# Self-attention in two row halves, the residual added by TensorE, and idle products on TensorE, in a three-stage transformer kernel

## The reference

```
x = x + cross_attention(context, layernorm(x))       # 16 heads of 16, masked by lengths
h = layernorm(x)
x = x + LN( h + softmax(causal(q k^T / 16) + bias) v @ proj + proj_b ) * ln_g + ln_b
g = layernorm(x)
x = x + down( qdq( qdq(g_gate * sigmoid(g_gate)) * g_up ) )  # weights in 4 bits by blocks of 32,
                                                             # activations in 16 bits by one scale
```

## Time and profile before

| | us |
|---|---|
| median of 3 runs (lowest, highest) | 1663.82 (1662.29, 1664.6) |
| the profiled execution | 1663.34 |
| its span in the trace | 1661.2 |
| TensorE busy, products | 1419.8 (85%) |
| VectorE busy | 1079.0 (65%) |
| ScalarE busy | 890.3 (54%) |
| GpSimd busy | 839.5 (51%) |

### The profile page before, as it was taken

How to read it: one execution, slowest core, us unless ns; L and a number is a source line. 1 busy time by engine, 2 the same in 40 slices (tenths; PEclk the granted TensorE clock), 3 DMA queues, 4 the chain that set the end, 5 groups by cost and what they waited for, 6 DMA issues and landing times. The chain is left out here.

```text
span 1661.2 us, 54781 instructions
## 1 busy us (share of the span) xinstructions
PE 1419.8 (85%) x24061; PEld 990.7 (60%) x24061; DVE 1079.0 (65%) x1743; ACT 890.3 (54%) x1170; POOL 839.5 (51%) x557
## 2 busy tenths in 40 slices
PE   4789999999999999999999999999975477448508
PEld 2357777776777777667777766777753255323207
DVE  7756666666666666666666666666633468885984
ACT  1446666565566655556665555666555244234752
POOL 5567666555666655556665556666302477211000
PEclk9899999999999999999999999999997678678859
DMA  5553354444344444433444443345303520010001
GB/s 169 128 143 102 102 122 124 110 129 124 102 102 121 122 116 115 135 102 103 117 123 116 115 139 102 102 117 126 73 14 110 138 54 9 1 38 1 0 0 52
DMA packets 91916, 158.55 MB, mean 95 GB/s; under 512 B 17488, under 2 KB 56280, under 8 KB 91680
## 3 DMA queue, kind: packets, MB, share of 16 engines
q1 hardware_dynamic: 90320, 154.07, 35.6%
q10 hardware_dynamic: 1360, 0.98, 0.2%
HBM read 60.95 MB, written 2.20 MB: 38 GB/s over the span
## 5 line engine op out<-in xcount | busy, mean ns | idle before, releaser
L638 DVE TENSOR_REDUCE MXP<-W_PS 128x1 f32<-128x512 f32 x768 | 499.1, 687 | 284.6 <-PE W_PS L450 284.6
L534 ACT ACTIVATE PR<-S_PS 128x1024 f32<-128x1024 f32 (+1 forms) x416 | 424.9, 1023 | 259.9 <-PE S_PS L398 252.0
L344 POOL TENSOR_TENSOR K_HI<-K,MCOL 128x512 f16<-128x512 f32 (+1 forms) x224 | 219.5, 980 | 426.7 <-ACT K L542 425.4
L346 POOL TENSOR_TENSOR K_LO<-K,K_HI 128x512 f16<-128x512 f32 (+1 forms) x224 | 291.9, 1303 | 17.6
L450 PE MATMUL W_PS<-STK,QS 105*128 105x512 f16 (+1 forms) x1024 | 269.8, 335 | 9.0 <-POOL STK L371 4.8
L398 PE MATMUL S_PS<-QS,STK 105*128 105x128 f16 (+1 forms) x3328 | 256.1, 220 | 1.0 <-DVE QS L652 1.0
L413 PE MATMUL O_PS<-PR,V 128*17 128x64 f32 x13312 | 231.3, 220 | 8.4 <-ACT PR L534 7.5
L413 PEld LDWEIGHTS O_PS<-PR,V 128*17 128x17 f32 x13312 | 190.8, 97 | 79.4 <-issue 59.3
L433 PE MATMUL W_PS<-WV_HI,CTX_HI 128*128 128x256 f16 (+1 forms) x832 | 228.3, 274 | 1.6 <-DVE WV_LO L611 1.4
L398 PEld LDWEIGHTS S_PS<-QS,STK 105*128 105x128 f16 (+1 forms) x3328 | 201.3, 99 | 45.3 <-issue 1.3
L433 PE MATMUL W_PS<-WV_HI,CTX_LO 128*128 128x256 f16 (+1 forms) x832 | 227.8, 274 | 0.0
(11 more groups left out here) (239 smaller groups left out, 1600.0 us busy)
## 6 DMA issues: line engine op xcount, KB each, us to landing
CTX<-in_ctx_t SPq DMA_DIRECT2D x64, 800.5 KB, 5.9
STK<-K_HI SPq DMA_DIRECT2D x256, 128.0 KB, 2.5
STK<-K_HI SPq DMA_DIRECT2D x256, 72.1 KB, 2.1
STK<-K_LO SPq DMA_DIRECT2D x128, 128.0 KB, 2.6
STK<-K_LO SPq DMA_DIRECT2D x128, 72.1 KB, 2.1
QSTK<-STK SPq DMA_DIRECT2D x12, 192.0 KB
V<-T SPq DMA_DIRECT2D x2, 1024.0 KB, 10.0
SQS<-QK_HI SPq DMA_DIRECT2D x32, 64.0 KB, 2.1
```

The lines of the kernel that those rows point to most:

```text
L344: pool.tensor_tensor(K_HI[:, m, lo:hi], k32, zero, ALU.add).then_inc(k_hi, 1)
L346: pool.tensor_tensor(K_LO[:, m, lo:hi], k32, K_HI[:, m, lo:hi], ALU.subtract).then_inc(k_lo, 1)
L534: nc.scalar.activation(PR[0:m, par, :], S_PS[par][0:m, :], ACT.Exp).then_inc(p_sb, 1)
L638: dve.tensor_reduce(MXP[:, j, at:at + 1], bank[:, :], AX.X, ALU.max).then_inc(mx_done, 1)
```

## The change

**Heads.** SQS and SKS have 128 rows. Transfers write every fourth row: rows q, q+4, ... hold part q of a head pair, so the even head lies in rows 0 to 63 and the odd one in rows 64 to 127; every fourth row from 3 on is zero. A block's scores are 32 products of 64 rows and 64 columns in place of 16 of 96 rows and 128 columns, and S_PS holds the even heads first. A round has 24 transfers. For round 0 ScalarE issues the eight with the keys' high part.

**Zeros.** Two transfers zero the rows of SQS and SKS; VectorE clears V by memsets; `zero_keys` goes.

**Values.** ScalarE copies V (`values`). VV of round 1 moves from SETUP to steps 1 and 2, QK, TN and WT units are spread anew.

**Residual.** TensorE adds it and the bias row: a product of the identity with XN, one of a row of ones with BP, then the projection. ScalarE copies the sum to XN behind the exponential of the step. GpSimd's four bias sums go.

**ScalarE's order.** Units come behind the exponential.

**Gate weight.** It has memory of its own (WN) and is loaded and prepared ahead of step 0.

**Norms.** Groups are 0 to 7, 8 to 12, 13 to 15. For blocks 0 to 7 ScalarE centres and scales (`centred`, steps 12 and 13), GpSimd multiplies by the weight (steps 13, 14) and VectorE adds four blocks at once (`add_weighted`).

**Idle products.** 12 ahead of SETUP, 8 ahead of the gate units and 8 ahead of the down projection, 400 columns each, results unused.

```diff
 SETUP = [
     ("TN", 0, 0), ("TN", 0, 1), ("QK", 0, 0), ("QK", 0, 1), ("QK", 0, 2), ("QK", 0, 3), ("TN", 1, 0), ("TN", 1, 1),
-    ("VV", 0, 0), ("VV", 0, 1), ("QK", 1, 0), ("QK", 1, 1), ("QK", 1, 2), ("QK", 1, 3), ("VV", 1, 0), ("VV", 1, 1),
+    ("VV", 0, 0), ("VV", 0, 1), ("QK", 1, 0), ("QK", 1, 1), ("QK", 1, 2), ("QK", 1, 3),
 ]
 BESIDE = {
-    0: [("TN", 2, 0), ("TN", 2, 1)], 1: [("QK", 2, 0), ("QK", 2, 1)], 2: [("QK", 2, 2), ("QK", 2, 3)],
-    3: [("TN", 3, 0), ("TN", 3, 1)], 4: [("QK", 3, 0), ("QK", 3, 1)], 5: [("QK", 3, 2), ("QK", 3, 3)],
-    6: [("VV", 2, 0)], 7: [("VV", 2, 1)], 8: [("WT", 0, 0), ("WT", 0, 1)], 9: [("WT", 0, 2), ("WT", 0, 3)],
-    10: [("VV", 3, 0)], 11: [("VV", 3, 1)],
-    16: [("XT", 0, 0), ("XT", 0, 1)], 17: [("XT", 1, 0), ("XT", 1, 1), ("XT", 2, 0)],
+    0: [("TN", 2, 0), ("TN", 2, 1)], 1: [("QK", 2, 0), ("VV", 1, 0)], 2: [("QK", 2, 1), ("VV", 1, 1)], 3: [("QK", 2, 2)],
+    4: [("QK", 2, 3), ("TN", 3, 0), ("TN", 3, 1)], 5: [("QK", 3, 0)], 6: [("QK", 3, 1), ("VV", 2, 0)], 7: [("QK", 3, 2), ("VV", 2, 1)],
+    8: [("QK", 3, 3)], 9: [("WT", 0, 0), ("WT", 0, 1)], 10: [("VV", 3, 0), ("WT", 0, 2)], 11: [("VV", 3, 1), ("WT", 0, 3)],
+    16: [("XT", 0, 0), ("XT", 0, 1)], 17: [("XT", 1, 0), ("XT", 1, 1)],
 }
-ENDING = [("XT", 2, 1), ("XT", 3, 0), ("XT", 3, 1)]
+ENDING = [("XT", 2, 0), ("XT", 2, 1), ("XT", 3, 0), ("XT", 3, 1)]
 STEPS = TILES + 3
 WIDE = 4
 NARROW = 2
-RESIDUAL = {0: 0, 1: 1, 4: 2, 7: 3}
-NORMS = [(0, 10), (10, 14), (14, 16)]
-ADDED = {13: (0, 1, 2), 14: (3, 4, 5), 15: (6, 7, 8), 16: (9,)}
+WARM = 12
+NORMS = [(0, 8), (8, 13), (13, 16)]
 CHAIN = 12
-AGGREGATED = [10, 20, 24, 28, 30, 32]
+AGGREGATED = [8, 16, 21, 26, 29, 32]
 ROOT_GUESS = 1597463007.0
-MAXIMA = [(0, 4), (4, 8), (8, 10), (10, 14), (14, 16)]
+MAXIMA = [(0, 4), (4, 8), (8, 13), (13, 16)]
...
-    SQS = alloc("SQS", [96, 2, PAIRS, CH], F16)
-    KZ = alloc("KZ", [96, 2, PAIRS, 2, CH], F16)
+    SQS = alloc("SQS", [P, 2, PAIRS, CH], F16)
+    SKS = alloc("SKS", [P, 2, PAIRS, CH], F16)
     T = alloc("T", [P, 3, PAIRS, 2, SQ], F32)
     MX = alloc("MX2", [P, 2, PAIRS, 2], F32)
     SM = alloc("SM2", [P, 2, PAIRS, 2], F32)
     PT = alloc("PT2", [P, 2, PAIRS, P], F32)
     OT = alloc("OT2", [P, 2, KT, P], F32)
+    WN = alloc("WN2", [P, WCOLS], F32)[:, :]
+    ONE = alloc("ONE", [1, P], F32)
...
+    zeroed = sem(nc, ctx, "zeroed")
+    PARTS = 24
...
+    def stack(eng, r, dst, q, part, m):
+
+        for c in range(4):
+            eng.dma_start(dst[q:P:4, r % 2, c::4, :], part[32 * c:32 * c + 32, r % 2, m:m + 2, :]).then_inc(stacked[r], 16)
...
+        sp.dma_start(WN.rearrange("p (f d) -> p f d", f=FT), dram["w_gate"].rearrange("(f p) d -> p f d", p=P)).then_inc(sm["in_wg"], 16)
         sp.wait_ge(sm["zero"], 1)
...
+        for home in (SQS, SKS):
+            sp.dma_start(home[3:P:4].rearrange("p u j c -> p (u j c)").bitcast(F32).rearrange("p (n z) -> p n z", n=4),
+                         ZERO[0:32].unsqueeze(1).broadcast_to([32, 4, PAIRS * 2 * SQ])).then_inc(zeroed, 16)
...
             sp.wait_ge(sm["qk_hi"], 4 * r + 2)
             if r >= 2:
                 sp.wait_ge(sm["s_ps"], 4 * (r - 1))
-            queries(0, QK_HI)
-            queries(1, QK_HI)
-            sp.wait_ge(sm["qk_hi"], 4 * r + 4)
-            if r == 0:
-                sp.wait_ge(sm["zero"], 5)
-            elif r == 1:
-                sp.wait_ge(zeroed[1], 32)
-            keys(0, QK_HI)
-            keys(2, QK_HI)
+            stack(sp, r, SQS, 0, QK_HI, 0)
+            stack(sp, r, SQS, 1, QK_HI, 0)
+            if r:
+                sp.wait_ge(sm["qk_hi"], 4 * r + 4)
+                stack(sp, r, SKS, 0, QK_HI, 2)
+                stack(sp, r, SKS, 2, QK_HI, 2)
+            sp.wait_ge(sm["qk_lo"], 4 * r + 2)
+            stack(sp, r, SQS, 2, QK_LO, 0)
             sp.wait_ge(sm["qk_lo"], 4 * r + 4)
-            queries(2, QK_LO)
-            keys(1, QK_LO)
-            if r == 1:
-                sp.wait_ge(sm["w_hi"], 1)
-                sp.wait_ge(sm["w_lo"], 1)
-                sp.dma_start(WN.rearrange("p (f d) -> p f d", f=FT), dram["w_gate"].rearrange("(f p) d -> p f d", p=P))\
-                    .then_inc(sm["in_wg"], 16)
+            stack(sp, r, SKS, 1, QK_LO, 2)
...
@@ -1031,27 +1008,30 @@
         def scores(t):
 
             r, lo = t // 4, t % 4 * P
+            if t == 0:
+                pe.wait_ge(zeroed, 32)
...
             for j in range(PAIRS):
                 for w in range(2):
                     cols = slice(lo + w * SQ, lo + (w + 1) * SQ)
-                    last = pe.matmul(S_PS[SQ * w:SQ * (w + 1), j * P:(j + 1) * P], SQS[0:96, r % 2, j, cols],
-                                     KZ[0:96, r % 2, j, :, cols], start=True, stop=True, skip_group_check=True)
+                    for a in range(2):
+                        rows = slice(64 * a, 64 * a + 64)
+                        last = pe.matmul(S_PS[SQ * w:SQ * (w + 1), 512 * a + j * SQ:512 * a + (j + 1) * SQ], SQS[rows, r % 2, j, cols],
+                                         SKS[rows, r % 2, j, cols], start=True, stop=True, skip_group_check=True)
             last.then_inc(sm["s_ps"], 1)
...
+        warm = CST[:, :].bitcast(F16)
+        for _ in range(WARM):
+            pe.matmul(T_PS[:, 0:400], warm[:, 0:P], warm[:, 0:400], start=True, stop=True, skip_group_check=True)
...
-        project(OT[:, 0]).then_inc(sm["bp_ps"], 1)
+        pe.wait_ge(sm["bp_row"], 2)
+        for g in range(KT):
+            last = pe.matmul(Y_PS[:, 0:D], OT[:, 0, g, :], WP[:, g, :], start=(g == 0), stop=(g == KT - 1))
+        last.then_inc(sm["bp_ps"], 1)
...
             if live(s - 3):
                 t = s - 3
                 if t == 0:
-                    pe.wait_ge(sm["bp_row"], 2)
+                    pe.wait_ge(sm["bp_row"], 3)
                 pe.wait_ge(sm["ot"], t + 1)
                 need(pe, sm["y_sb"], t)
-                project(OT[:, t % 2]).then_inc(sm["y_ps"], 1)
+                pe.matmul(Y_PS[:, 0:D], CST[:, C_ID:C_ID + P], XN[:, t, :], start=True, stop=False)
+                pe.matmul(Y_PS[:, 0:D], ONE[0:1, :], BP[0:1, :], start=False, stop=False)
+                for g in range(KT):
+                    last = pe.matmul(Y_PS[:, 0:D], OT[:, t % 2, g, :], WP[:, g, :], start=False, stop=(g == KT - 1))
+                last.then_inc(sm["y_ps"], 1)
...
+                if r == 0 and i == 3:
+                    act.wait_ge(sm["qk_hi"], 4)
+                    stack(act, 0, SKS, 0, QK_HI, 2)
+                    stack(act, 0, SKS, 2, QK_HI, 2)
+            elif kind == "VV":
+                values(x)
...
+        def values(x):
...
+            for a in range(2):
+                rows = slice(SQ * a, SQ * (a + 1))
+                nc.scalar.activation(V[rows, r % 2, 4 * i:4 * i + 4, :, DH * a:DH * (a + 1)],
+                                     bank[rows, :].rearrange("p (b j d) -> p b j d", b=4, j=PAIRS), ACT.Copy, scale=1 / W_SCALE)\
+                    .then_inc(sm["v_sb"], 1)
...
+            for t in tiles:
+                nc.scalar.activation(XN[:, t, :], XN[:, t, :], ACT.Identity, bias=VT[:, t:t + 1], scale=RS[:, t:t + 1])\
+                    .then_inc(sm["xz"], 1)
...
@@ -1159,27 +1162,33 @@
                 if t == 0:
                     act.wait_ge(sm["bp_ps"], 1)
                 nc.scalar.activation(OT[:, t % 2, :, :], O_PS[:, 0:D].rearrange("p (g r) -> p g r", g=KT), ACT.Copy).then_inc(sm["ot"], 1)
-            for x in BESIDE.get(s, []):
-                if x[0] != "XT":
-                    setup(x)
             if live(s):
                 act.wait_ge(sm["t_sub"], s + 1)
                 nc.scalar.activation(T[:, s % 3], T[:, s % 3], ACT.Exp, scale=1 / 16).then_inc(sm["t_exp"], 1)
-            if s == 16:
+            if live(s - 3):
+                t = s - 3
+                act.wait_ge(sm["y_ps"], t + 1)
+                nc.scalar.activation(XN[:, t, :], Y_PS[:, 0:D], ACT.Copy).then_inc(sm["y_sb"], 1)
+            if s == 12:
+                act.wait_ge(sm["chain"], CHAIN)
+                centred(range(0, 4))
+            if s == 13:
+                centred(range(4, 8))
+            if s == 15:
                 act.wait_ge(sm["chain"], CHAIN * 2)
                 normal_again(range(0, 4))
-            if s == 17:
-                normal_again(range(4, 10))
+            if s == 16:
+                normal_again(range(4, 8))
             for x in BESIDE.get(s, []):
-                if x[0] == "XT":
-                    setup(x)
+                setup(x)
         act.wait_ge(sm["chain"], CHAIN * 4)
-        normal_again(range(10, 14))
+        normal_again(range(8, 13))
         setup(ENDING[0])
         setup(ENDING[1])
         act.wait_ge(sm["chain"], CHAIN * 6)
-        normal_again(range(14, 16))
+        normal_again(range(13, 16))
         setup(ENDING[2])
+        setup(ENDING[3])
...
-            if s in RESIDUAL:
-                r = RESIDUAL[s]
-                pool.wait_ge(sm["bp_row"], 2)
```

(66 more changed lines are left out.)

98 lines of the change are left out of this document (29 added, 69 removed).

## The result

| | before | after |
|---|---|---|
| median (lowest, highest) | 1664.21 (1662.29, 1665.7) | 1655.6 (1653.13, 1656.54) |
| the profiled execution | 1663.34 | 1654.98 |
| its span | 1661.2 | 1653.1 |

The ratio is 0.9947, its 95% interval 0.9931 to 0.9962: faster by 8.6 us, where 20 were forecast, and 0.6 us above the upper end of the range. Five windows of the trace after answer to the earlier trace rows; the columns are the same (TensorE, its weight loads, VectorE, ScalarE, GpSimd, granted clock, DMA share, GB/s).

What follows compares the result with a forecast made beforehand. Before step 0 two waits in series (stacking, V's zeros) bound the kernel, in the steps a chain across engines. Step 0 23.3 us sooner, 3.5 lost behind it, feed-forward 0: net -19.8 from 1663.34, so 1643.5 us, range 1631 to 1655.

Steps and rivals of the forecast that it cites:

- signs of being wrong: Said to refute the forecast: steps running at 5 us or at 8, or ScalarE's transfers taking more than 0.7 us each.
- Part 1: Way to step 0: waits for stacking and V's zeros go; step 0 starts at 1281.5, 23.3 us sooner, bounds 1276 to 1284.
- Part 2: Steps 0 to 12 of self-attention: 97.6 us at full clock against 97.5 before, so the steps do not get shorter.
- the chain: Steps from 3 on: sum, maximum, subtraction, exponential, ScalarE's projection copy and statistics in series, 6.3 us a step.
- Part 3: Step 13 to the layer's end: steps 13 and 14 take 26.1 us (before 25.7), the rest 41.7 (before 45.3).
- The clock: Behind the start of step 0: half-clock passages add 6 to 10 us, 6.5 taken, giving 172 us.
- Part 4: Feed-forward: idle products ahead of gate and down projection worth 0; bounds a gain of 1.3 + 1.9, a loss of 2.
- (D): Steps: ScalarE the new bound, late V copies add 1 to 1.5 us in ten steps; 1653 to 1658; chance 0.15.
- (B): Steps and tail: identity products keep TensorE at 2.4 GHz; 1637, or 1632 with cheap ScalarE issues; chance 0.2.
- (C): Feed-forward: idle products take the whole 3.2 us of half clock off gate and down projection; 1640; chance 0.05.
- (E): Steps: doubled projection at half clock sets them, 8.1 us without a unit, 12.8 with one; 1685, slower; chance 0.03.
- (F): Way to step 0: another wait keeps step 0 near 1300; 1662, no difference; chance 0.02.

Runs made afterwards that it cites:

- norm_early: The changed kernel, but VectorE normalises blocks 8 to 15 ahead of the gate weight's maximum, where GpSimd is idle: 1654.0 us.
- sp_keys: norm_early, but SyncE issues all 24 transfers of round 0 and ScalarE none: 1652.3 us.
- fill: The changed kernel with more idle products, ahead of each PV's wait and of TensorE's longer waits: 1649.9 us.
- copy_dve: The changed kernel, but VectorE, not ScalarE, copies the projection's sum to XN, just ahead of the statistics: 1656.0 us.
- one_product: The changed kernel without the product of the ones row with the bias: 1641.4 us.
- residual_dve: The changed kernel with the residual back on VectorE and the bias sums on GpSimd, no identity or ones product, no ScalarE copy: 1641.1 us.
- fill_tail: fill, with the 40 idle products ahead of block 15's transposition gone and 70 ahead of block 14's: 1646.5 us.
- v_late: The changed kernel, but ScalarE copies the values of a step's V unit in the next step: 1650.3 us.
- no_idle: The changed kernel without any idle product ahead of the setup, gate units or down projection: 1654.9 us.
- act_first: The changed kernel with ScalarE's units ahead of the exponential, as in the kernel before: 1697.8 us.

## Why the prediction was wrong

The span came out 11.7 us longer than forecast (1653.1 against 1661.2 less 19.8): 3.1 us ahead of step 0, 0.65 in the feed-forward, and the rest behind step 0, above all steps 0 to 12 with 109.1 us for 97.6. Two of the prediction's own signs of being wrong came true: steps of 8 us, and transfers of more than 0.7 us on ScalarE.

**Part 1** was right in kind (both waits gone) and 3 us too early, outside its bounds. The failed term is VectorE's: its TN parts were given 1284 at worst by the memsets' length (1.76 us each, within the 1.2 to 2.4 taken), and nothing for the eight normalisations that come to stand beside GpSimd's mask and gate weight (7.68 us for 2.7). ScalarE's issue was bounded by 0.65 us a transfer and is 0.80, beyond the end taken. One trace each puts the two at 1.1 and 1.6 us of step 0's start (norm_early, sp_keys). The scores (0.44 us) were cheaper than 0.6.

**Part 2** holds the main error. Nine of the thirteen lengths were within 0.5 us for a kernel at full clock: fill shows 8.6, 3.8, 4.2, 10.6, 11.3, 6.2, 6.6, 8.1, 8.1, 7.6, 9.2, 12.3, 6.2 against 8.2, 3.8, 4.2, 10.2, 10.1, 6.3, 6.3, 7.2, 7.6, 7.9, 8.2, 11.3, 6.3. The four misses of about 1 us are steps 4, 7, 10 and 11, which have two or three units. "At full clock it ends just ahead of the exponential" took the doubled projection as covered. In steps with few units and full clock it is (6.2 us in steps 5 and 12 of fill), and the 8.1 given for half clock is what step 12 took (8.05); in the others the list of TensorE is the step, and the added 1.25 us (1344.23 to 1345.48 in the rows of step 7) were to be added to it, not laid beside the chain. The conclusion, "the steps do not get shorter: what leaves VectorE is replaced by the chain", named the wrong cause for the kernel as it runs: copy_dve opens the chain and gains nothing, one_product takes one product out, leaves the chain, and gains 14.2 us; residual_dve takes out both products and the chain for 14.5. The chain itself was sized rightly (6.2 for 6.3) but sets only those steps in which TensorE is done sooner.

**Part 3** was right for steps 13 and 14 (25.7 us, forecast 26.1) and 3.6 short for the end (45.8 against 42.2: the 41.7 of the prediction and the 0.5 us between its mark 1473.35 and VectorE's 1473.85). Of this fill_tail gives 2.1 to the half clock, and residual_dve, without the two products, takes 2.6 off; the two overlap, since the products too run at half clock there. PV, the three products and the transposition of the last blocks lie one behind the other there.

**The clock.** 6.5 us were taken for all that follows step 0. The traces show 3 to 6 in steps 0 to 12 and 2 at the end. The size is about right; but it is not a sum that one adds: it is owed in the steps that TensorE's list sets, here nearly all of those with units, in residual_dve and its kin still step 10 with 2.3 us.

**Part 4** was right: both idle groups in the feed-forward are worth nothing, the distances are those of before but for one gate unit at half clock.

**The rivals.** (D) gave 1653 to 1658, and 1655.6 was measured. Its mechanism (a V copy ahead of the transposed block's) is in the rows, at 0.2 to 0.3 us in steps 7 and 8 where it gave 1 to 1.5 in ten steps; v_late's median, 5.3 us lower, is the most that it can be given. The number was right by luck, in the main for another reason. (B) fell: 0.84 of the clock. (C) fell by no_idle (feed-forward 188.0 us with and without). (E) was given 0.03; its step of 8.1 us is step 12 (8.05), and act_first, at 1697.8, shows how near the kernel stands to it. (F) fell. No rival held what was decisive: that the kernel with the residual left where it was would be faster (1641.1), by two products of TensorE that the sum counted and laid beside other work.

## What to carry to other kernels

Work moved to an engine with idle time is free only in the steps in which that engine waits: add the moved instructions to its list step by step, with its heaviest units, before laying them beside the chain. A clock at half costs time in those steps that TensorE's list sets, and a kernel can keep such a step when the others hang on something else, so ask step by step. Idle products must end before the work that they precede: much the same ones gave 5.7 us in one kernel and none in its neighbour, where 40 of them held up the scores. An instruction that only moves within an engine's list can still change its length: VectorE's normalisations took 0.33 us alone and 0.96 beside GpSimd. And before taking a start time for the gain of an edit, see how far it varies between traces of one order: here 2 us.

## What the hardware showed

- A float32 product of one row (ones, L1057) takes TensorE as long as one of 128 rows (identity, L1056): 0.69 and 0.70 us at full clock, both 1.22 at half. The Trainium skill (TensorE: Matmul & The Clock Gate, Why this matters for your kernels) says that a single product over 32 rows takes the time of one over 128; the trace agrees, down to one row.
- Normalising 256 columns took VectorE 0.33 us alone and 0.96 beside GpSimd.
- Eight stack transfers take ScalarE's queue 6.1 to 7.0 us to issue (6.42 after, 6.10 norm_early, 6.95 res_fill), SyncE's 5.2 to 6.6 (5.16 to 6.35 after, up to 6.58 in residual_dve).
- 32 score products of 64 rows and 64 columns in two row halves take 0.44 us at full clock and 0.64 at half; 16 of 96 rows and 128 columns took 0.64 and 1.06 before.
